# Cross attention: the transposed input made a step sooner in two buffers, packed keys ahead of the maxima, context keys and transposed z later in the fourth step

## The reference

```
x = x + attn(layernorm(x))      # causal, 16 heads of 64, own layernorm
x = x + xattn(layernorm(x), ctx_2048)
x = x + ffn(layernorm(x))       # 8 experts, top 2, capacity
```

```
qkv = (x @ w_qkv.T).reshape(B, N, 3, H, D).transpose(2, 0, 3, 1, 4)   # H = 16, D = 8
extra_k, extra_v = context as (2, B, H, N_c, D)
k = concatenate([extra_k, k], axis=2);  v = concatenate([extra_v, v], axis=2)
attn = softmax(einsum('bhnd,bhmd->bhnm', q * D ** -0.5, k))
out = einsum('bhnm,bhmd->bhnd', attn, v).reshape(B, N, C) @ w_proj.T + b_proj
```

## Time and profile before

| | us |
|---|---|
| median of 3 runs | 1139.82 (1139.49 to 1140.05) |
| the profiled execution, its own time | 1140.01 |
| its span | 1138.1 |
| granted TensorE clock, mean over the span | 0.983 |
| cross attention in steady course | about 476 to 802 |

### The profile page before, as it was taken

One profiled execution on the slowest core, in us unless ns is written; L12 is line 12 of the kernel. 1 busy time (PEld: TensorE's weight loads), 2 busy tenths in 40 slices (PEclk: granted clock), 3 DMA queues, 4 the chain that ended last, 5 costly groups with the idle time before them and its releaser, 6 DMA issues.

```text
span 1138.1 us, 32254 instructions
## 1 busy us (share of the span) xinstructions
PE 1038.3 (91%) x12779; PEld 769.4 (68%) x12779; DVE 868.7 (76%) x2002; ACT 700.1 (62%) x1543; POOL 458.4 (40%) x799
## 2 busy tenths in 40 slices
PE   5899999999999996989889888888866999999997
PEld 4688888878888775666666666666643666666664
DVE  5888778887788875677777777777747788888887
ACT  2666666666666664666666666666644755555554
POOL 3444444444444453244344354454332422222222
PEclk9999999999999999899999999999987999999999
DMA  7000000000000000000000000003000000000000
GB/s 172 2 2 2 2 2 2 2 2 2 2 2 2 2 1 11 11 16 12 12 15 12 13 14 11 16 11 96 28 1 1 1 11 10 11 10 11 11 11 11
DMA packets 20666, 16.11 MB, mean 14 GB/s; under 512 B 7043, under 2 KB 18597, under 8 KB 20517
## 3 DMA queue, kind: packets, MB, share of 16 engines
q1 hardware_dynamic: 20176, 13.90, 4.6%
q10 hardware_dynamic: 340, 0.14, 0.1%
HBM read 11.94 MB, written 2.10 MB: 12 GB/s over the span
## 4 chain that ended last, share of the span: by engine, by line
DVE 42%; PE 26%; issue 21%; POOL 6%; ACT 2%; DMA 1%; DVEq 0%; SPq 0%; POOLq 0%; ACTq 0%
PE ps L1027 24%; DVE nmax L865 8%; DVE nmax L687 6%; POOL probs L514 6%; DVE rsum L694 5%; DVE zT L720 3%; DVE kT L737 3%; DVE raw_gu L732 2%; DVE kT L824 2%; DVE q_part L824 1%; DVE rinv L697 1%; DVE xT L704 1%; DMA wv<-in_L_attn_W_v 1%; DVE bst L884 1%; DVE bst L891 1%
## 5 line engine op out<-in xcount | busy, mean ns | idle before, releaser
L865 DVE TENSOR_REDUCE nmax<-ps 128x2 f32<-128x512 f32 x256 | 163.7, 682 | 46.3 <-PE ps L1027 45.2
L625 ACT ACTIVATE probsT<-ps 128x512 f32<-128x512 f32 x256 | 139.5, 601 | 54.8 <-PE ps L1027 52.5
L552 ACT ACTIVATE probs<-ps,nmax 128x128 f32<-128x128 f32 x512 | 142.9, 382 | 10.6 <-DVE nmax L687 10.6
L514 POOL TENSOR_TENSOR probs<-wk,probs 128x512 f16<-128x512 f32 x64 | 74.0, 1156 | 185.8 <-ACT probs L668 182.9
L1027 PE MATMUL ps<-probsT,va 128*32 128x128 f32 x2048 | 137.1, 276 | 5.3 <-ACT zT L630 5.3
L399 POOL TENSOR_TENSOR probs<-probs,rinv 128x512 f32<-128x512 f32 x128 | 133.1, 1040 | 18.1 <-DVE rinv L697 18.1
L546 ACT COPY probsT<-ps 128x512 f32<-128x512 f32 x128 | 75.1, 587 | 100.5 <-PE ps L1078 100.4
L660 ACT ACTIVATE wq<-ps 128x512 f32<-128x512 f32 x128 | 76.5, 598 | 72.4 <-PE ps L1027 72.2
L1027 PEld LDWEIGHTS ps<-probsT,va 128*32 128x32 f32 x2048 | 103.5, 110 | 23.3 <-issue 16.3
L687 DVE TENSOR_REDUCE nmax<-ps 128x4 f32<-128x512 f32 x128 | 83.4, 672 | 38.2 <-PE ps L1027 38.2
L1011 DVE TENSOR_TENSOR probs<-wk,probs 128x512 f16<-128x512 f32 x64 | 71.9, 1123 | 43.8 <-ACT probs L668 43.8
(11 more groups left out here) (220 smaller groups left out, 2633.5 us busy)
## 6 DMA issues: line engine op xcount, KB each, us to landing
ctx_row<-in_ctx SPq DMA_DIRECT2D x32, 128.0 KB, 2.0
out_x<-x_all SPq DMA_DIRECT2D x8, 256.0 KB, 2.3
kT<-in_L_ffn_down_proj_w SPq DMA_DIRECT2D x1, 1024.0 KB, 10.9
wq<-in_L_attn_W_q SPq DMA_DIRECT2D x1, 512.0 KB, 4.9
wk<-in_L_attn_W_k SPq DMA_DIRECT2D x1, 512.0 KB, 9.4
wv<-in_L_attn_W_v SPq DMA_DIRECT2D x1, 512.0 KB, 10.3
wo<-in_L_attn_W_o SPq DMA_DIRECT2D x2, 256.0 KB, 6.1
x_all<-in_x SPq DMA_DIRECT2D x1, 256.0 KB, 3.3
```

The lines of the kernel that those rows point to most:

```text
L514: nc.gpsimd.tensor_tensor(h_lo[:, e % 2, 0, :], hT[:, 0, :], h_hi[:, e % 2, 0, :], ALU.subtract).then_inc(hidden_low_first, 1)
L552: last = nc.scalar.activation(probs[:, u, i * P:(i + 1) * P], ps[u][:, i * P:(i + 1) * P], ACT.Exp, bias=nmax[:, u, i:i + 1])
L625: last = nc.scalar.activation(probsT[:, 2 * (t % 2) + a, :], ps[2 + a][:, :], ACT.Exp)
L865: last = nc.vector.reduce_max(nmax2[:, b % 2, t:t + 2, l + a], ps[a][:, :].rearrange("p (t k) -> p t k", t=2), AX_X, negate=True)
```

## The change

`xT2_hi` and `xT2_lo` get two buffers, chosen by the batch's parity. The code of several steps moves:

- GpSimd: the normalisation to xn2 is written under g == 1 instead of g == 2.
- TensorE: the transpose of xn2 goes from g = 3 to g = 2, behind that of xn3 and ahead of scores(2), without the wait for the halves of the batch before. The context keys go from g = 2 to g = 3, behind v. The logits product and the transpose of zn go from ahead of scores(3) to behind the transposed scores of g = 3; they now wait for `ca_xT_taken` of the same step.
- VectorE: the pack of the keys goes ahead of maxima(1). The copy of xT3 waits for xn2's transpose as well. `xT2_lo` is made at the end of g = 2, and the copies of z and the logits at the end of g = 3, behind the maxima.
- ScalarE: `xT2_hi` is made at the end of g = 2, behind exponentials(2); the context keys are copied in g = 3, behind v.

The diff, cut to its core:

```diff
-        xT2_hi = sb("xT2_hi", [P, P], F16)
-        xT2_lo = sb("xT2_lo", [P, P], F16)
+        xT2_hi = sb("xT2_hi", [P, 2, P], F16)
+        xT2_lo = sb("xT2_lo", [P, 2, P], F16)
...
@@ GpSimd @@
-                    if g == 2 and valid(2):
+                    if g == 1 and valid(2):
...
@@ ScalarE @@
-                    if g == 2 and valid(1):
+                    if g == 3 and valid(1):
                         n = b + 1
                         act.wait_ge(ca_keys_in_bank, n + 1)
...
-                    if g == 3 and valid(2):
+                    if g == 2 and valid(2):
                         act.wait_ge(ca_xT_in_bank, b + 3)
                         if valid(-3):
-                            act.wait_ge(logits_in_bank, b - 2)
-                        if valid(-2):
-                            act.wait_ge(ca_zT_in_bank, b - 1)
-                        nc.scalar.activation(xT2_hi[:, :], ps[7][:, 0:P], ACT.Copy, scale=X2_SCALE).then_inc(ca_xT_high, 1)
+                            act.wait_ge(ff_xT_taken, b - 2)
+                        nc.scalar.activation(xT2_hi[:, parity, :], ps[7][:, 0:P], ACT.Copy, scale=X2_SCALE).then_inc(ca_xT_high, 1)
...
@@ VectorE @@
                         dve.wait_ge(ff_xT_in_bank, n + 1)
+                        if valid(2):
+                            dve.wait_ge(ca_xT_in_bank, b + 3)
...
+                    if g == 2 and valid(2):
+                        dve.wait_ge(ca_xT_high, b + 3)
+                        nc.vector.scalar_tensor_tensor(out=xT2_lo[:, parity, :], in0=ps[7][:, 0:P], scalar=X2_SCALE,
...
@@ TensorE, self-attention @@
-                        if not valid(1):
-                            pe.wait_ge(ca_xT_taken, 1 if valid(0) else 2)
+                        if not valid(2):
+                            pe.wait_ge(ca_xT_taken, 1 if valid(1) else 2)
...
@@ TensorE, cross attention @@
+                    if g == 2 and valid(2):
+                        pe.wait_ge(ca_norm, b + 3)
+                        if not valid(0):
+                            pe.wait_ge(sa_residual, NB + b - 1)
+                        nc.tensor.transpose(ps[7][:, 0:P], xn2[:, :], ident[:, :]).then_inc(ca_xT_in_bank, 1)
...
                     if g == 3:
                         if valid(-3):
                             pe.wait_ge(ff_xT_taken, b - 2)
                         if valid(2):
-                            pe.wait_ge(ca_norm, b + 3)
...
-                            if valid(1):
-                                pe.wait_ge(ca_xT_taken, n + 1)
-                            nc.tensor.transpose(ps[7][:, 0:P], xn2[:, :], ident[:, :]).then_inc(ca_xT_in_bank, 1)
+                            pe.wait_ge(ca_xT_taken, b + 3)
```

More of the change, by code:

```diff
@@ L844, in cross_attention @@
                         nc.vector.tensor_copy(xT3[:, :], ps[7][:, 2 * P:3 * P]).then_inc(ff_xT_taken, 1)
[L845 to L859, removed]
+                    if g == 1 and valid(1):
+                        n = b + 1
+                        dve.wait_ge(ca_k_subgh, n + 1)
+                        pack(kT2[:, n % 3, :, P:KEYS2], k_sub[:, :, :],
+                             ps[5][:, :].rearrange("p (t q) -> p t q", t=4)).then_inc(ca_k_packed, 1)
                     if valid(0):
@@ L1240, in cross_attention @@
                         last.then_inc(ca_zq_in_bank, 1)
-                    if g == 2 and valid(1):
+                    if g == 2 and valid(-3):
+                        pe.wait_ge(ff_norm, b - 2)
+                        pe.wait_ge(ca_residual, b - 2)
+                        nc.tensor.transpose(ps[7][:, 2 * P:3 * P], xn3[:, :], ident[:, :]).then_inc(ff_xT_in_bank, 1)
+                    if g == 2 and valid(2):
[3 more added lines that the diff above has]
+                        nc.tensor.transpose(ps[7][:, 0:P], xn2[:, :], ident[:, :]).then_inc(ca_xT_in_bank, 1)
+                    if g == 3 and valid(1):
+                        if valid(-2):
+                            pe.wait_ge(ca_normalised, b - 1)
+                        else:
+                            pe.wait_ge(ca_q_packed, n + 1)
+                        for k, (xs, w) in enumerate(((xT2_hi, w2_hi), (xT2_hi, w2_lo), (xT2_lo, w2_hi))):
+                            last = mm(ps[near][:, 0:P], xs[:, n % 2, :], w[:, 2, :], k == 0, k == 2)
+                        last.then_inc(ca_v_in_bank, 1)
+                    if g == 3 and valid(1):
                         pe.wait_ge(ca_context_keys, n + 1)
@@ L1247, in cross_attention @@
                         last.then_inc(ca_keys_in_bank, 1)
[L1248 to L1259, removed]
+                    if valid(0):
+                        scores(b, g)
+                    if g == 0 and valid(-2):
+                        apply_values(b - 2, UNITS - 1)
+                    if valid(-1):
+                        transposed_scores(b - 1, g)
                     if g == 3:
@@ L1275, in cross_attention @@
                                                 ident[:, :]).then_inc(ca_zT_in_bank, 1)
-                    if valid(0):
-                        scores(b, g)
-                    if g == 0 and valid(-2):
-                        apply_values(b - 2, UNITS - 1)
-                    if valid(-1):
-                        transposed_scores(b - 1, g)
-                        if g > 0:
-                            apply_values(b - 1, g - 1)
+                    if valid(-1) and g > 0:
+                        apply_values(b - 1, g - 1)
             pe.wait_ge(const_ready, 9)
```

33 lines of the change are left out of this document (18 added, 15 removed).

## The result

| | before | changed |
|---|---|---|
| median | 1139.65 us (1139.31 to 1140.05) | 1188.58 us (1185.56 to 1190.14) |
| profiled execution | 1140.01 us | 1189.46 us |
| granted TensorE clock, mean over the span | 0.983 | 0.957 |

The ratio is 1.0428, with a 95% interval of 1.0413 to 1.0443. The change costs 49 us; the forecast was +15, and its range ended at 1165. The direction was right, the size was not.

A forecast was written before the change was run, and what follows sets the result against it. The prediction took a loop through GpSimd's late xn2 to set a 12.65 us interval against 12.06: 1140.01 + 15.9 - 1 = 1154.9, or 1154.7 us for the median. Range 1146 to 1165, some 80%.

The forecast's parts named there:

- What bounds the kernel, and the 27 intervals: Cross attention's chain of waits: one batch per 12.06 us interval, batches 3 to 29, so any effect counts 27 times.
- By itself this part trades one wait for another: Packing keys ahead of maxima(1): the 0.65 us wait goes, but scores(2) begin at 633.33, about when they do now.
- Xn2 reaches TensorE at 634.24: GpSimd starts xn2 at 633.38, 2.72 after 630.66; its transpose on TensorE follows 0.86 us later.
- The loop: From xn2's transpose through scores, maxima, aggregate and GpSimd to the next transpose: 12.65 us against 12.06, +15.9 us in all.
- 5.38: Loop term on TensorE, scores(2) to next scores(0): 5.86, less 0.59 wait, plus 0.22 context keys, less 0.11 moved transpose.
- By the spans: Timing GpSimd by 3.09 us busy instead of starts 3.48 us apart: interval 0.44 shorter, 12.21 us, 1143 us in all.
- The covers that I called thin or absent: Spare time before other TensorE waits: 0.07 us before scores(3), none at the logits product; these links were costed at nothing.
- The clock: TensorE's granted clock behind the new wait: a drop was held unlikely, as the wait stays under 1.7 us.
- Slower, and more: Rival: thin covers are missing or TensorE's clock drops; interval 12.95 to 13.3 us, 1163 to 1173 us; chance 8%.
- The edges: Batches outside the 27 intervals, joined batches included: bounded by -2.5 and +1.5 us, taken as -1.
- The rival "faster": Xn2 stands in SBUF by 633.0, so the loop runs over k_sub: 11.53 us interval, 1124.5 us; chance 8%.
- No change: Rival: waits trade evenly on TensorE, the busiest engine; interval stays 12.06 us, 1140 us in all; chance 4%.

The follow-up runs named there:

- the filled ones: The changed kernel with 24, 12 or 6 unused TensorE products between the transposes of xn3 and xn2: 1163.96, 1165.99 and 1184.77 us.

## Why the prediction was wrong in size and right in direction

**What bounds the kernel, and the 27 intervals:** right; 46.9 of the 49.5 us lie in them.

**"By itself this part trades one wait for another":** wrong, by the run with the pack alone: a gain of 6 us there, a loss where the statistics are out of the way, and nothing in the changed kernel, where the second half of the sentence holds and xn2 covers it. It did no harm to the sum.

**Xn2 reaches TensorE at 634.24, by GpSimd's starts and not by its spans:** right. The loop measures, from the transpose at 645.06 to that at 657.95 and term by term as in the prediction: 0.26 (said 0.21), 5.57 (5.38), 0.43 (0.44), 2.67 (2.66), 0.38 (0.38), 2.71 (2.72), 0.87 (0.86), the sum 12.89 (12.65). By the spans it would have been 12.21. The rule of the Trainium skill, Perfetto Trace Analysis, section "GPSIMD Engine Instruction", to time this engine by start-to-start spacing, is borne out: from the first variance to xn2 the starts are 2.71 apart in the new loop, as they were 2.72 apart before, while the durations of the five instructions in between sum to 2.36.

**The mis-sized terms of the loop:** 5.38 should have been 5.57, and this is all of what is missing but 0.05. The four context-key products were priced at 0.22 by the earlier trace rows. They take 0.32 in the new place (647.04 to 647.36), and in the unmoved place they take 0.33 when nothing is waited for ahead of them, as in the run with early statistics and pack ahead, on TensorE:

```profile
640.60 0.39 PE L1027 MATMUL ps<-ident_h,keys 128*128 128x128 f16 x4
640.93 0.33 PE L1251 MATMUL ps<-ident,xn 128*128 128x128 f32 x1
```

The 0.22 was read right behind a wait of 0.65. Why the products stand closer there stays open. The logits with zn's transpose were priced at 0.38 and take 0.49 (647.90 to 648.39). The covers that I called thin or absent did hold, since TensorE has no listed wait at scores(3) or at the logits. These terms are worth 0.24 x 27 = 6.5 us.

**The clock: the step that failed.** In "Slower, and more" I wrote that a new wait under 1.7 us with the engine busy most of the rest made a fallen clock unlikely. The forecast put the clock at nothing. The wait was in the foreseen bounds, 1.45, and the clock fell to half in about every second interval, here and in the variants with 1.45 or 1.11 us of this wait: 24.7 of the 49 us. The only row I judged by was a wait of 2.59, and one case above tells nothing about cases below. The trace of before had a nearer case that I overlooked. In its joined batches TensorE idles 1.13 us before 434.78 and 1.46 before 436.89, and the clock goes from 1.00 to half behind them:

```profile
436.89 0.38 PE L1027 MATMUL ps<-ident_h,keys 128*128 128x128 f16 x4 [1.46 <-DVE kT L824]
```

```profile
436.00:438.00 2.00, 0.77 (x8) 0.66 (x8) 1.91 (x4) 2.00 (x7) 1.81 (x5) 1.00 0.00 0
438.00:440.00 2.00, 1.55 (x15) 1.22 (x14) 1.50 (x4) 1.47 (x4) 1.92 (x5) 0.51 0.04 8
```

I gave this rival 8%. Its size, 1163 to 1173, was too low as well. One fall costs 1.55, and one in every second interval 27 / 2 x 1.55 = 21 us; the fall of 17.26 adds 4.4 by itself. How often the clock would fall in the new order no row of before tells, so the upper end of the range should have stood open towards an interval at half clock throughout its products, and it did not.

**The edges:** I took -1, and they are +2.6: +1.5 in front (1.42 of it by the output product of self-attention, 448.84 instead of 447.42) and +1.1 at the end, whose cause stays open. The prediction gave GpSimd 4.46 us of idle to wait for the moved context-key product. That holds in the steady course; in the joined batches the last L399 stands right behind those copies, and TensorE waits for it. I named another wait there, the output product's for xT2_lo; it is 0.5 us.

**The rival "faster"** had the right path and the right condition, an xn2 that is in time. That its 11.53 stands so near the measured 11.55 is luck: two misses cancel. From scores(0) to scores(2) it gave 6.15 (4.03 + 0.68 + 1.29 + 0.15) and 5.98 was measured, because from the start of the pack it took 1.95 to scores(2) (640.50 to 642.45) and not 2.12; the second half it gave as 5.38 and 5.56 was measured.

**"No change"** by the most-contended engine fell: TensorE has the same work in all of these kernels but the filled ones, and their times go from 1118 to 1189. That TensorE is the busiest engine was weak ground too: its 91% are products in flight, which overlap, and its weight loads are busy 68%, less than VectorE's 76%.

## What to carry to other kernels

When a step is moved forward, find the queue that makes its input: here GpSimd made xn2 in the second half of a row of six instructions, and moving the consumer past that bought nothing but a wait; giving xn2 and its statistics the first place turned +4.3% into -0.9%. Do this at the edges of a stage as well, where other work shares the list. Price a new idle stretch of TensorE twice, once as the time itself and once as products at half clock behind it, and count it for each repetition. And before the order across engines is changed, look at the engine that releases the bounding one for work that is not needed yet: two instructions that held the maxima up by 0.57 us, moved into an idle of the same engine, were worth 16 us alone.

## What was not expected of the hardware

The granted clock fell to half with a wait of 1.45 us once in an interval of 12.89, and with 1.11 us, and stayed at full with 0.78. It did not fall at each such wait but at about every second one. It was low from 658 to shortly before 662 in the interval shown, and in one (17.26) from 600 to 610. Products whose results nobody needs gave 24.6 us back.

A product that waits for maxima of VectorE started 0.06 after their end (641.08 to 641.14 with the pack alone moved), not 0.15 as behind the pack.
